# A mixture-of-experts layer computed for each token's two chosen experts only, on one core

## The reference, cut to what matters

```python
mod = (silu(c) @ wmod).reshape(8, 6, 1, 128)           # sa, ca, ga, sb, cb, gb for each of 8 sequences
h = layernorm(x) * (1 + ca) + sa                       # x: (8, 256, 128)
...                                                    # scores of all 256 tokens; the best 128, in order: tok
n1 = ln(tok); u, res = split(n1 @ m_in_w)              # 128 -> 512
tok = tok + (u' * s[:, None] * silu(res)) @ m_out_w    # s from u' @ m_xproj_w
n2 = ln(tok)
rw, sel_e = top_k(softmax(n2 @ moe_r_w + moe_r_b), 2)  # 2 of 8 experts
gate = zeros(N, 8).at[..., sel_e].add(rw / rw.sum(-1))
h1 = gelu(einsum('nd,edh->enh', n2, moe_w1) + moe_b1)  # every expert, 128 -> 512
eo = einsum('enh,ehd->end', h1, moe_w2) + moe_b2       # 512 -> 128
tok = tok + einsum('end,ne->nd', eo, gate)
x = x + ga * (h with tok * w put back in its rows)
h = layernorm(x) * (1 + cb) + sb
# FFN, 128 -> 352 -> 128, on inputs, weights and hidden values rounded to FP4 in blocks of 16
x = x + gb * fp4_linear(silu(fp4_linear(h, w_gate)) * fp4_linear(h, w_up), w_down)
```

## Time and profile before

| | us |
|---|---|
| median of 3 runs | 284.91 (283.39 to 285.16) |
| span of the profiled execution, first to last instruction | 281.4 |
| median of the runs less that span | 3.5 |
| busy in the span: PE / DVE / ACT / POOL | 227.3 / 183.7 / 110.6 / 71.5 |

### The profile page before, as it was taken

How to read it: one execution, slowest core, us unless ns; L and a number is a source line. 1 busy time by engine, 2 the same in 40 slices (tenths; PEclk the granted TensorE clock), 3 DMA queues, 4 the chain that set the end, 5 groups by cost and what they waited for, 6 DMA issues and landing times.

```text
span 281.4 us, 3576 instructions
## 1 busy us (share of the span) xinstructions
PE 227.3 (81%) x1181; PEld 161.3 (57%) x1181; DVE 183.7 (65%) x571; ACT 110.6 (39%) x229; POOL 71.5 (25%) x86
## 2 busy tenths in 40 slices
PE   2481779968999999999899999998899892567470
PEld 2330755544767787847677658684575591544360
DVE  1698856447898873556588957958668627886610
ACT  2437125345357753276244363233625400222210
POOL 5220010173311010057011141142131122244252
PEclk9977597977999997999999999999999998595755
DMA  7990004311000000001000000000000000000000
GB/s 219 365 362 9 0 2 159 142 38 40 0 0 0 2 1 0 2 17 48 12 0 0 3 0 20 2 1 19 0 21 0 1 2 19 0 19 0 19 19 19
DMA packets 8113, 11.13 MB, mean 40 GB/s; under 512 B 1104, under 2 KB 4248, under 8 KB 8096
## 3 DMA queue, kind: packets, MB, share of 16 engines
q1 hardware_dynamic: 7072, 8.82, 9.5%
q0 software_dynamic: 1024, 2.10, 2.6%
HBM read 9.85 MB, written 1.06 MB: 39 GB/s over the span
## 4 chain that ended last, share of the span: by engine, by line
PE 51%; DVE 30%; ACT 8%; issue 4%; POOL 4%; DMA 1%; DVEq 0%; SPq 0%; ACTq 0%; POOLq 0%
PE aux_ps L896 19%; PE down_ps L896 13%; PE up_ps L896 12%; DVE q_am L655 3%; PE small_ps L896 3%; ACT qb L444 2%; DVE stats L605 2%; DVE hh L870 2%; DVE acc L828 2%; POOL rstd L394 2%; DVE hh L866 2%; DVE qa L660 2%; DVE q_ri L659 2%; DVE wide L660 1%; ACT hT L486 1%
## 5 line engine op out<-in xcount | busy, mean ns | idle before, releaser
L896 PEld LDWEIGHTS down_ps<-w_s,h1T 128*128 128x128 f32 x512 | 61.6, 194 | 10.0 <-issue 9.1
L896 PE MATMUL up_ps<-n2T,w_s 128*128 128x512 f32 x128 | 65.4, 627 | 1.5 <-ACT h1T L539 1.5
L896 PE MATMUL down_ps<-w_s,h1T 128*128 128x128 f32 x512 | 63.7, 279 | 1.4 <-issue 0.8
L539 ACT ACTIVATE h1T<-up_ps,par 128x512 f32<-128x512 f32 x64 | 43.2, 685 | 29.5 <-PE up_ps L896 28.7
L394 POOL TENSOR_TENSOR rstd<-veps,half_pow 128x4 f32<-128x4 f32 (+2 forms) x11 | 12.1, 1099 | 95.5 <-DVE veps L610 95.5
L896 PEld LDWEIGHTS up_ps<-n2T,w_s 128*128 128x128 f32 x128 | 22.1, 197 | 24.7 <-ACT h1T L539 15.1
L896 PE MATMUL aux_ps<-w_guT,h2T 128*128 128x352 f32 x64 | 24.2, 516 | 4.0 <-ACT h2T L561 3.6
L828 DVE SCALAR_TENSOR_TENSOR acc<-down_ps,gate,acc 128x128 f32<-128x128 f32 x64 | 18.0, 343 | 11.8 <-PE down_ps L896 11.5
L444 ACT ACTIVATE qb<-qa 128x704 f32<-128x704 f32 (+3 forms) x7 | 4.7, 671 | 41.5 <-DVE qa L660 41.5
L896 PE MATMUL aux_ps<-w_dnT,hqT 128*128 128x128 f32 (+1 forms) x96 | 16.2, 333 | 5.9 <-ACT hqT L581 5.9
L896 PEld LDWEIGHTS aux_ps<-w_guT,h2T 128*128 128x128 f32 x64 | 12.8, 212 | 12.9 <-ACT h2T L561 4.5
(11 more groups left out here) (172 smaller groups left out, 334.3 us busy)
## 6 DMA issues: line engine op xcount, KB each, us to landing
w_s<-moe_w_dram SPq DMA_DIRECT2D x16, 256.0 KB, 6.6
mod_r<-mod_dram SPq DMA_DIRECT2D x1, 2048.0 KB, 7.5
hx<-x_dram SPq DMA_DIRECT2D x2, 512.0 KB, 5.4
wmod_s<-wmod_dram SPq DMA_DIRECT2D x1, 384.0 KB, 3.9
w_in_s<-w_in_dram SPq DMA_DIRECT2D x1, 256.0 KB
w_gu_s<-w_gu_dram SPq DMA_DIRECT2D x2, 128.0 KB, 7.7
xp<-x_dram,row_ix POOLq DMA_INDIRECT x16, 2.5
out_dram<-yo,row_ix POOLq DMA_INDIRECT x16, 2.2
```

Of the source, the lines that this page charges most:

```text
L539: nc.scalar.activation(h1T[:, m % 2, hc, :], up_ps[(m * HC + hc) % UP_BANKS][:], ACT.Gelu, bias=col("moe_b1", i)).then_inc(up_done, 1)
L896: return nc.tensor.matmul(o, lhsT=l, rhs=r, start=start, stop=stop)
```

## The change

Each group's tokens are copied (scattered) twice, to a place in a buffer in DRAM (`xs_dram`) in which every expert has whole tiles of 128 rows; 512 tokens times 2 and 8 experts need at most 15 tiles (`XT`), and 15 are always computed. PE counts each token's place among its expert's (`slots`, small bf16 matmuls), DVE turns that into row numbers, tile owners (`tile_e`) and two gates per token, POOL scatters the normalised rows with 8 indirect DMAs, SP loads them back (`xT`, 4 loads), PE transposes, ACT applies ln2's weights. For each of the 15 tiles SP reads the expert's number into a register and loads that expert's 526 KB (w1, w2 and b1 in one row of `w_e`, 4 slots), PE does 4 matmuls of 128 columns, ACT 4 gelus of 128x128, PE 4 matmuls, ACT copies the result to `ys`. SP stores `ys` (`yst`), POOL gathers two rows per token with 8 indirect DMAs (`comb`), and DVE adds them with their gates in 8 instructions. Both scatter buffers are zeroed by DMA at the start. `ORDER` becomes five lists, one for each engine; the sets are in a new order; `quantise` is split into a first part (..qa) and a second (..qb) so that other work can stand between, with `qb` and `hh` doubled; `ln_h`, `norm` and `ffn_in` are split in the same manner (`st..` moments, `nm..` normalise), and `ln_h`'s moments are first of all on DVE for both groups. Waits on `small_ps` are by one new counter (`small_taken`). h2T, hqT and ffa get second buffers. The reload of `mod_r` stands on SP behind `xT.0.0`.

```diff
+XT = (2 * GT + E * (P - 1)) // P
...
+QUADS = [(q, min(4, XT - q)) for q in range(0, XT, 4)]
+EW = HID + HC * D + HC
...
+MOE_BANKS = 3
+WSLOTS = 4
...
-SETS = [(0, 1, 0, BG), (0, 0, 0, BG), (1, 1, 0, BG), (1, 0, 0, BG // 2), (1, 0, BG // 2, BG // 2)]
+SETS = [(0, 1, 0, BG), (1, 1, 0, BG), (0, 0, 0, BG), (1, 0, 0, BG // 2), (1, 0, BG // 2, BG // 2)]
...
+ORDERS = {
+    "PE": """
+        modh.0.0 modh.1.0 hT.0.0 hr.0.0 srow.0.0 scol.0.0 place.0.0 perm.0.0 mod.0.0 soft.0.0 n1.0.0 inproj.0.0
+        mix.0.0 attn.0.0 hT.1.0 hr.1.0 srow.1.0 n2.0.0 logits.0.0 slots.0.0 gateT.0.0 bias2.0.0 scol.1.0
+        place.1.0 perm.1.0 soft.1.0 n1.1.0 wqT.0.0 inproj.1.0 xT.0.0 mix.1.0 attn.1.0 xT.0.1 up.0.0-1 xT.0.2
+        down.0.0 n2.1.0 down.0.1 logits.1.0 up.0.2 xT.0.3 up.0.3 slots.1.0 down.0.2 up.0.4 gateT.1.0 up.0.5
+        down.0.3-4 up.0.6 down.0.5 up.0.7 bias2.1.0 down.0.6 h2T.0.0 gu.0.0-2 down.0.7 up.0.8 gu.0.3 up.0.9
+        down.0.8 up.0.10 hqT.0.0 down.0.9 dn.0.0 up.0.11-12 down.0.10 hqT.0.1 down.0.11 up.0.13 dn.0.1 down.0.12
+        xT.1.0 up.0.14 xT.1.1 down.0.13 up.1.0 xT.1.2 up.1.1 down.0.14 h2T.1.0 xT.1.3 gu.1.0-1 up.1.2 gu.1.2
+        down.1.0-1 up.1.3 gu.1.3 hqT.1.0 down.1.2-3 up.1.4 dn.1.0 down.1.4 up.1.5 hqT.1.1 down.1.5 up.1.6-7
+        dn.1.1 down.1.6 up.1.8-9 down.1.7-8 h2T.2.0 down.1.9 gu.2.0-2 up.1.10-11 gu.2.3 down.1.10 up.1.12
+        down.1.11 hqT.2.0 up.1.13-14 down.1.12-14 hqT.2.1 dn.2.0-1 h2T.3.0 gu.3.0-1 h2T.4.0 gu.4.0-1 hqT.3.0
+        dn.3.0 hqT.4.0 dn.4.0
+""",
+    "ACT": """
+        silu.0.0 modh.0.0 modh.1.0 hT.0.0 hr.0.0 srow.0.0 scol.0.0 perm.0.0 exps.0.0 n1.0.0 inproj.0.0 hT.1.0
+        hr.1.0 n2.0.0 logits.0.0 srow.1.0 wqa.0.0 gateT.0.0 scol.1.0 exps.1.0 wqa.0.1 perm.1.0 n1.1.0 wqT.0.0
+        inproj.1.0 xT.0.0 up.0.0-1 xT.0.1-2 n2.1.0 down.0.0-1 logits.1.0 up.0.2-3 down.0.2 xT.0.3 up.0.4
+        gateT.1.0 down.0.3-4 up.0.5-6 fqa.0.0 h2T.0.0 down.0.5 gu.0.0-1 up.0.7 down.0.6 gu.0.2 down.0.7 gqa.0.0
+        up.0.8 gu.0.3 down.0.8 up.0.9 hqT.0.0 gqa.0.1 up.0.10 down.0.9 up.0.11 down.0.10 hqT.0.1 up.0.12-13
+        down.0.11-12 xT.1.0 up.0.14 fqa.1.0 down.0.13 up.1.0 xT.1.1 down.0.14 h2T.1.0 xT.1.2-3 gu.1.0-1 up.1.1
+        gu.1.2 down.1.0 gqa.1.0 up.1.2 down.1.1 gu.1.3 up.1.3 hqT.1.0 down.1.2 gqa.1.1 up.1.4 down.1.3-4 up.1.5
+        hqT.1.1 down.1.5 up.1.6-7 down.1.6 fqa.2.0 up.1.8 down.1.7 up.1.9 h2T.2.0 gu.2.0-1 down.1.8 gu.2.2
+        down.1.9 up.1.10 gqa.2.0 up.1.11 gu.2.3 up.1.12 down.1.10 hqT.2.0 down.1.11 up.1.13-14 gqa.2.1
+        down.1.12-14 hqT.2.1 fqa.3.0 h2T.3.0 gu.3.0 fqa.4.0 gu.3.1 h2T.4.0 gu.4.0-1 gqa.3.0 gqa.4.0 hqT.3.0
+        hqT.4.0
+""",
+    "DVE": """
+        silu.0.0 sth.0.0 sth.1.0 nmh.0.0 nmh.1.0 scol.0.0 place.0.0 smax.0.0 rank.0.0 perm.0.0 st1.0.0 nm1.0.0
+        mod.0.0 bc.0.0 soft.0.0 inproj.0.0 mix.0.0 attn.0.0 st2.0.0 nm2.0.0 wqa.0.0 logits.0.0 slots.0.0
+        scol.1.0 wqa.0.1 bias2.0.0 place.1.0 smax.1.0 rank.1.0 perm.1.0 wqb.0.0 st1.1.0 wqb.0.1 nm1.1.0 soft.1.0
+        stf.0.0 inproj.1.0 mix.1.0 attn.1.0 st2.1.0 nm2.1.0 logits.1.0 slots.1.0 fqa.0.0 fqb.0.0 bias2.1.0
+        gu.0.0-1 gqa.0.0 gu.0.2 gqb.0.0 gu.0.3 gqa.0.1 gqb.0.1 dn.0.0 stf.1.0 dn.0.1 fqa.1.0 fqb.1.0 gu.1.0-1
+        gqa.1.0 gu.1.2 gqb.1.0 gu.1.3 gqa.1.1 comb.0.0 gqb.1.1 stf.2.0 dn.1.0 fqa.2.0 dn.1.1 fqb.2.0 gu.2.0-1
+        gqa.2.0 gqb.2.0 gu.2.2-3 gqa.2.1 gqb.2.1 dn.2.0-1 comb.1.0 stf.3.0 stf.4.0 fqa.3.0 fqb.3.0 fqa.4.0
+        gu.3.0 fqb.4.0 gu.3.1 gqa.3.0 gu.4.0-1 gqb.3.0 gqa.4.0 gqb.4.0 dn.3.0 dn.4.0
+""",
+    "POOL": """
+        sth.0.0 sth.1.0 st1.0.0 gather.0.0 st2.0.0 slots.0.0 wqb.0.0 st1.1.0 wqb.0.1 gather.1.0 stf.0.0 st2.1.0
+        slots.1.0 fqb.0.0 gqb.0.0-1 stf.1.0 dn.0.0 out.0.0 dn.0.1 fqb.1.0 comb.0.0 gqb.1.0 out.0.1 gqb.1.1
+        stf.2.0 dn.1.0 out.1.0 fqb.2.0 dn.1.1 gqb.2.0 out.1.1 gqb.2.1 comb.1.0 dn.2.0-1 out.2.0-1 stf.3.0
+        stf.4.0 fqb.3.0 fqb.4.0 gqb.3.0 gqb.4.0 dn.3.0 out.3.0 dn.4.0 out.4.0
+""",
+    "SP": """
+        xT.0.0 mod.0.0 fetch.0.0-1 xT.0.1 fetch.0.2 xT.0.2-3 fetch.0.3-12 xT.1.0-1 yst.0.0 xT.1.2 yst.0.1 xT.1.3
+        fetch.0.13-14 yst.0.2 fetch.1.0-2 yst.0.3 fetch.1.3-6 yst.1.0 fetch.1.7-9 yst.1.1 fetch.1.10-14
+        yst.1.2-3
+""",
+}
...
-        w1_s = sb("w1_s", [P, E, HID])
-        w2_s = sb("w2_s", [P, E, HC, D])
+        w_e = sb("w_e", [P, WSLOTS, EW])
...
+                elif kind == "fetch":
+                    n = g * XT + i
+                    sp.wait_ge(tile_e_ready, g + 1)
+                    if n >= WSLOTS:
+                        sp.wait_ge(down_full, n - WSLOTS + 1)
+                    e = sp.value_load(tile_e[0:1, g, i:i + 1], min_val=0, max_val=E - 1)
+                    sp.dma_start(w_e[:, n % WSLOTS, :], moe_w[bass.ds(e * P, P), :]).then_inc(ld_we[n % WSLOTS], 16)
+                elif kind == "xT":
+                    t, n = QUADS[i]
+                    sp.wait_ge(scattered[g], 2 * BG * 16)
+                    sp.dma_start(ys[:, g, t:t + n, :], xs_dram[g][t * P:(t + n) * P, :].rearrange(
+                        "(t p) d -> p t d", p=P)).then_inc(ld_xs[i], 16)
+                elif kind == "yst":
+                    t, n = QUADS[i]
+                    sp.wait_ge(ys_ready, g * XT + t + n)
+                    sp.dma_start(ys_dram[g][t * P:(t + n) * P, :].rearrange("(t p) d -> p t d", p=P),
+                                 ys[:, g, t:t + n, :]).then_inc(ys_stored[g], 16)
...
+                elif kind == "slots":
+                    pool.wait_ge(zeroed, NG * 16)
+                    pool.wait_ge(slot_ix_ready, g + 1)
+                    for c in range(2 * BG):
+                        nc.gpsimd.indirect_dma_start(
+                            out=xs_dram[g][:, :], out_offset=bass.IndirectOffsetOnAxis(
+                                ap=slot_ix[:, g, c // BG, c % BG:c % BG + 1], axis=0),
+                            in_=xd[:, g, c % BG, :], in_offset=None).then_inc(scattered[g], 16)
+                elif kind == "comb":
+                    pool.wait_ge(ys_stored[g], len(QUADS) * 16)
+                    for c in range(2 * BG):
+                        nc.gpsimd.indirect_dma_start(
+                            out=ys[:, g, c, :], out_offset=None, in_=ys_dram[g][:, :],
+                            in_offset=bass.IndirectOffsetOnAxis(ap=slot_ix[:, g, c // BG, c % BG:c % BG + 1], axis=0)
+                        ).then_inc(combined[g], 16)
...
+                elif kind == "xT":
+                    t, n = QUADS[i]
+                    wait_aux_full(act, kind, g, i, 0)
+                    if g > 0:
+                        act.wait_ge(up_full, (g - 1) * XT + t + n)
+                    nc.scalar.activation(xsT[:, t * P:(t + n) * P], aux(kind, g, i, 0)[:, 0:n * P], ACT.Identity,
+                                         scale=col("ln2_w"), bias=col("ln2_b")).then_inc(aux_taken(kind, g, i, 0), 1)
                 elif kind == "up":
+                    n = g * XT + i
+                    if n >= 2:
+                        act.wait_ge(down_full, n - 1)
+                    act.wait_ge(up_full, n + 1)
+                    act.wait_ge(ld_we[n % WSLOTS], 16 * (n // WSLOTS + 1))
+                    for hc in range(HC):
+                        at = HID + HC * D + hc
+                        last = nc.scalar.activation(h1T[:, n % 2, hc, :], moe_ps[n % MOE_BANKS][:, hc, :], ACT.Gelu,
+                                                    bias=w_e[:, n % WSLOTS, at:at + 1])
+                    last.then_inc(up_done, 1)
+                elif kind == "down":
+                    n = g * XT + i
+                    act.wait_ge(down_full, n + 1)
+                    nc.scalar.activation(ys[:, g, i, :], moe_ps[n % MOE_BANKS][:, 0, :], ACT.Copy).then_inc(ys_ready, 1)
...
+                    dve.wait_ge(slots_full, g + 1)
+                    cum = small_ps[:, g, 128:128 + BG * E].rearrange("p (t e) -> p t e", e=E)
+                    tot = small_ps[:, g, 160:160 + E]
...
+                    V.tensor_scalar(slot_ix[:, g, 0, :], ends[:, 0, :], FAR, None, ALU.add)
+                    V.tensor_scalar(slot_ix[:, g, 1, :], ends[:, 1, :], FAR, None, ALU.subtract
+                                    ).then_inc(slot_ix_ready, 1)
+                    link(V.tensor_tensor(end, base, count, ALU.add))
...
+                    V.tensor_scalar(tile_e[:, g, :], small[:, 14:16, :].rearrange("p a c -> p (a c)"), E - 1.0, None,
+                                    ALU.min).then_inc(tile_e_ready, 1)
+                    for k in range(2):
+                        link(V.tensor_tensor(pos[:, 0, :, :], pos[:, 1 + k, :, :],
+                                             ends[:, k, :].unsqueeze(2).broadcast_to([P, BG, E]), ALU.is_equal))
+                        link(V.tensor_tensor(pos[:, 0, :, :], pos[:, 0, :, :], gate[:, g, :, :], ALU.mult))
+                        link(V.reduce_sum(g2[:, g, k, :], pos[:, 0, :, :], AX_X))
+                elif kind == "comb":
+                    dve.wait_ge(combined[g], 2 * BG * 16)
```

(52 more changed lines are left out.)

532 lines of the change are left out of this document (305 added, 227 removed).

## The result

The changed kernel took 288.7 us (286.4 to 289.5, four runs), the kernel before beside it 285.0 (283.4 to 285.6): a ratio of 1.013, interval 1.008 to 1.019. The forecast was 275.5. Its range of 262 to 290 holds the time; its direction is wrong. Five later executions of the same program beside others gave 288.4 against 284.4, ratio 1.014 (1.009 to 1.020). Times are medians of all executions of a kernel; the ratios leave out executions over 1.5% above the fastest of the same kernel.

A forecast was written before the change was run, and what follows sets the result against it. PE looked like the bound, but with no engine but DVE then near full the sum followed DVE's order: 71 + 62 + 77.5 + 16.5 + 45 = 272, plus 3.5, 275.5 us, 3% faster; range 262 to 290.

The forecast's parts named there:

- gate ready: In the front: the gate, ready at 65.1 us before, comes at 66.6 through small additions of 0.3 to 0.4.
- end of `slots.0` to `gu.0.0`: From group 0's row numbers at 71 us to set 0's first gu at 133: 46 of work, 16 of waits.
- `gu.0.0` to T: From set 0's first gu to T, the end of set 2's last rounding: 63.5 work, 14 waits, ending at 210.5.
- T to the end of `comb.1`: After set 2's last rounding: scaling, gathers and landing 14 us bare, then 2.4 for the sum, ending at 227.
- rest: After `comb.1`'s sum: the last two FFN sets without two dn of set 2, 45 us where 47.2 were.
- The 3.5 us: Added to the summed 272 because the runs' median is 3.5 above the profiled execution of 281.4.
- The reload of mod_r: On SP behind xT.0.0: lands at 91 to 92, DVE needs it for `stf.0` at about 94, 2 us of cover.
- (1): From 71 us on, the lists let DVE reach `gqb.2.1` with half its 30 us of waits: 263 us; chance 0.18.
- (2): Fetch and tile slots set the pace, deciding from 3.4 us a tile; at 4.0 the total is 293; chance 0.15.
- (3): Each scatter or gather on POOL waits for one DVE instruction of 0.89: 14 us on the path, 289; chance 0.04.
- (4): PE's clock falls in the middle, 1 us more in each of a dozen handoffs: 282 us; chance 0.13.
- (5): Expert tiles: work isn't saved where tokens crowd on one expert; 15 are always computed and already summed; no chance given.

The follow-up runs named there:

- h0: The changed kernel itself run again, nothing altered, beside the kernel before: 288.4 us, ratio 1.014.
- k1: The changed kernel with its five lists reordered behind the first slots and three front moves undone, no instruction changed: 268.2 us, ratio 0.944.
- h2: The changed kernel with SyncE's list alone changed, xT.1 loads ahead of fetch.0.11 and two stores between fetches: 285.2 us, ratio 0.999.
- f4: The changed kernel without the 32 indirect DMAs of scatter and gather, SyncE moving rows in plain order instead: 276.9 us, ratio 0.955.
- f3: The changed kernel with only the first four weight fetches, the other 26 tiles using whatever weights lie there: 284.9 us, ratio 0.992.
- h1: The changed kernel with 250 throwaway PE products filling gaps, nothing of the computation changed: 288.0 us (282.0 to 293.6).
- h3: The kernel before, own order, no routing, with PE's expert work cut to what the changed kernel has: 285.6 us, ratio 1.004.
- m1: The changed kernel, its own lists, with every up and down product of every tile made twice: 310.8 us, ratio 1.092.

## Why the prediction was wrong, step by step

Lengths in us, by the prediction's own marks; the changed kernel in its first profile and in h0.

| step | predicted | first profile | h0 | k1 |
|---|---|---|---|---|
| gate ready | 66.6 | 70.3 | 66.0 | 67.6 |
| end of `slots.0` to `gu.0.0` | 62 | 65.0 | 64.4 | 63.6 |
| `gu.0.0` to T | 77.5 | 87.4 | 88.4 | 76.6 |
| T to the end of `comb.1` | 16.5 | 15.4 | 15.4 | 8.8 |
| rest | 45 | 45.5 | 46.9 | 46.7 |

**The step that failed** is "from `gu.0.0` to the last rounding of set 2": 63.5 of work and 14 of waits. Work came to 67.0: DVE busy 64.3 and 2.7 us in the small gaps between linked instructions. 4.8 of it are three instructions and two groups of four stretched beside POOL (1.76 for 0.69 twice, 1.61 for 1.14 twice, 1.92 for 0.19). I had taken the pair's 6.86 from 136.98 to 144.69 of before, where POOL was idle until 144.75. Waits came to 20.4 (27.0 in the list, less the 6.6 ahead of the stretch): over the forecast are 1.7 at `dn.0.1`, 1.15 at `gu.0.1`, 1.7 at the last rounding, 0.8 for POOL's power, and smaller ones. The prediction's "most are now covered by another set's step" was too kind. Of this, h2 shows 3 us to be SyncE's list. k1 shows that the sum itself could be had: 76.6 with the same instructions. So what failed is the wait term, which I priced as if the lists were used at their best, and a work term taken from an undisturbed pair.

**The front** was right at +1.5: h0 has +0.9. The first profile's +5.2 goes with its lower clock (0.76 for 0.82). **`slots.0` to `gu.0.0`**: 6.1 to 6.6 us for tanh in one piece where I had 5, the rest in hand-offs. **`comb.1` bare**: 14 forecast, 13.0 measured, and f4 and k1 show it on the path. **The 3.5 us** added at the end are more than what lies around an execution: the profiled one of the changed kernel took 289.5 for its span of 287.8, so 1.7; the rest was the profiled execution of before being quicker than its median. **The reload of mod_r** was a near thing: issued at 87.4 and landed by 95, 3 us later than forecast with the gate; DVE reached `stf.0` at 97.3 and didn't wait. **PE 165 to 175 busy** was 187, at a clock I had not charged for; DVE 178 to 183 and POOL 100 to 108 held (182.0, 104.5).

**Rivals.** (1) Better filled: false for the change's lists, and what k1 is. (2) The tiles bind: half right. They pass in 3.9 us each (109.9 to 225.6 for 30), above the 3.4 at which I said the lists would feel it, but held by the lists and hardly by fetches: 3.8 in f3 without them, 3.3 in k1 with them. (3) The lock: a gather or scatter took 0.99 to 1.01 us on average, so POOL was hardly locked out. I had taken the lock in one direction only; it held DVE too, by 4.8 us in the middle (last section). (4) The clock: it fell as described, 0.76 and 0.91 for 0.93 and 1.00 of the earlier trace rows, and cost 1 or 2 us in the tail and a varying 0 to 4 in the front; the 282.0 of h1 leaves room for more. The Trainium skill (TensorE: Matmul & The Clock Gate, What's actually happening) says that an idle PE is throttled; the traces agree in the main: 0.61 where PE was busy for 34% of the changed kernel's last stretch, 0.97 where it was busy for 82%; but h3 has 0.77 at 80% and 0.86 at 73%. k1 shows that this alone decides little: the fastest kernel here has the lowest clock of all from 61 to 125. (5) is not touched by any run.

And the wider error: the 50 us of DVE's waits that I read as the room for a gain are not room that a lighter PE opens by itself. h3 took half of the experts' products from PE in the kernel before, and the waits stayed (52 us for 51), at a lower clock. I had put only 6 or 7 of PE's 55 us down to DVE's waits; what I did not do was ask of each remaining wait which list entry stands in front of it on each of the three engines that it runs through.

## What to carry to other kernels

A busy share of 95% doesn't make an engine the bound where every engine has a fixed list: shorten its work in the old order first and look at the next engine's waits. If they stay, look at the order and at the clock, and change work and order together (here the same PE work made 22 us in one set of lists and 41 in another). Where the new form also brings costs of its own, as the 26 us here, do the old work in it once, to see the two apart. Price a change by its own lists: for each wait, name what stands ahead of it on every engine of the hand-off; and place a block that needs a queue for 10 us where its input is ready and its user far off.

## What the runs showed of the hardware that was not expected

**DVE and POOL hold each other.** POOL's timeline beside the two slow DVE rows above:

```profile
155.01 1.39 POOL L466 TENSOR_TENSOR hx<-wide,q_sc 128x704 f32<-128x704 f32 x1 [5.02 <-DVE wide L772]
...
184.39 0.94 POOL L498 DMA_INDIRECT ys<-ys_dram,slot_ix  x1 [0.30 <-issue]
185.36 1.39 POOL L466 TENSOR_TENSOR hx<-wide,q_sc 128x704 f32<-128x704 f32 x1
```

A DVE product of two SBUF inputs that began 0.2 us into POOL's took 1.76 us for 0.69, and ended 0.5 after POOL's; an instruction of 0.19 took 1.92, until the second of POOL's, at 185.4, had ended. The first kind stands in f4 too (1.76 at 153.6), the second doesn't (0.19). POOL lost less: its worst gather took 1.55 for 0.94, beside a DVE rounding that had begun 0.2 us before it, and a product at 193.1 took 1.70 for 1.39. The Trainium skill (SBUF — State Buffer, SBUF: two separate sides) describes the port pair that the two share as a lock: whichever starts first has it for its whole instruction, and the other waits. The traces agree in both directions. The kernel before had a case too, which the prediction didn't look at:

```profile
71.22 1.50 POOL L383 TENSOR_TENSOR w_gu_s<-wide,q_sc 128x768 f32<-128x768 f32 x1 [4.62 <-DVE wide L664]
```

```profile
71.72 1.03 DVE L656 TENSOR_SCALAR q_sc<-q_am 128x22 f32<-128x22 f32 x1
```

DVE's row ends at 72.75, POOL's at 72.72; in the changed kernel the same instruction takes 0.18 at 80.7.

**The end of a program grows with its indirect DMAs.** The last one ends at 280.7 of 287.8 in the changed kernel, 278.1 of 285.2 in h0 and 260.4 of 267.4 in k1: 7.0 to 7.1 us to the end, with 64 such DMAs in the program. In the kernel before, in f4 and in h3, with 32, it is 4.4 (277.0 of 281.4, 272.0 of 276.4, 280.6 of 285.0). The last transfers are the same; that it is the count is argued from these six, not tried by itself.

**The same front, 4 us apart.** The front's program is the same in both profiles of the changed kernel, in f3, h2, f4 and m1, and its gate came at 70.2, 65.8, 66.4, 66.7, 68.3 and 69.0. What differs between the first two is the granted clock after the first waits of PE: from 18 to 28 us it is 0.67 in one and 0.84 in the other, and the same records of four products took 3.62 and 2.39 us. A step-by-step comparison of two profiles has to allow for that before it blames an order.
